# GpSimd's multiplication of q and k in four parts, three of VectorE's small steps in another order, and the values product in two pieces instead of three

## The reference

```python
x = x + 0.5 * ffn(layernorm(x))
x = x + attn(layernorm(x))
x = x + 0.5 * ffn(layernorm(x))

def attn(x):                                   # 16 heads of 64
    q, k, v = x @ Wq, x @ Wk, x @ Wv           # k and v get 4 memory rows in front
    q, k = l2norm(q), l2norm(k)
    dots = mix_heads(W_pre_th, q @ k.T * 10)   # a 16x16 mix over the heads
    dots = causal mask, then keep the 64 largest of each row
    attn = mix_heads(W_post_th, softmax(dots))
    out = (attn @ v) * head_scale * sigmoid(x @ Wg + bg)
    return out @ Wo
```

## Time and profile before

| | |
|---|---|
| median of 3 runs | 2192.57 us (2191.74 to 2193.78) |
| profiled execution, its own time | 2195.78 us |
| its span in the trace | 2194.0 us |
| busy in the span | PE 1996.8 (91%), PEld 1309.2, DVE 1698.7 (77%), ACT 1593.3 (73%), POOL 929.8 (42%) |
| mean granted TensorE clock | 0.963 of full speed |

### The profile page before, as it was taken

One profiled execution on the slowest core, in us unless ns is written; L12 is line 12 of the kernel. 1 busy time (PEld: TensorE's weight loads), 2 busy tenths in 40 slices (PEclk: granted clock), 3 DMA queues, 4 the chain that ended last, 5 costly groups with the idle time before them and its releaser, 6 DMA issues. The chain is left out here.

```text
span 2194.0 us, 56191 instructions
## 1 busy us (share of the span) xinstructions
PE 1996.8 (91%) x16059; PEld 1309.2 (60%) x16060; DVE 1698.7 (77%) x7474; ACT 1593.3 (73%) x4620; POOL 929.8 (42%) x2739
## 2 busy tenths in 40 slices
PE   6996689989998998999899989998999999984997
PEld 3433456676666666766666666666666766672433
DVE  6565389968996899689968986899699869964456
ACT  4442579967996899689868986898699778952542
POOL 3000555455545554555455546544664465321000
PEclk9997799999999999999999999999999999996998
DMA  6002012202220222112211221121122212202002
GB/s 185 3 0 91 12 48 52 62 16 53 64 53 24 53 65 46 28 46 65 46 27 46 65 46 27 46 65 46 28 54 57 46 28 64 68 15 92 0 1 77
DMA packets 113228, 104.82 MB, mean 48 GB/s; under 512 B 34448, under 2 KB 110864, under 8 KB 112912
## 3 DMA queue, kind: packets, MB, share of 16 engines
q1 hardware_dynamic: 108000, 96.65, 17.3%
q10 hardware_dynamic: 4912, 4.46, 0.6%
HBM read 19.14 MB, written 12.71 MB: 15 GB/s over the span
## 5 line engine op out<-in xcount | busy, mean ns | idle before, releaser
L1063 PE MATMUL bankC<-R,E 128*128 128x128 f32 x2560 | 347.9, 285 | 43.4 <-POOL R L1430 43.3
L1063 PEld LDWEIGHTS bankC<-R,E 128*128 128x128 f32 x2560 | 332.5, 199 | 82.5 <-POOL R L1430 49.3
L1047 PE MATMUL bankB<-raw,mixpre 128*128 128x76 f32 (+37 forms) x1024 | 339.5, 425 | 9.8 <-DMA raw<-SC 9.8
L1528 DVE TENSOR_SCALAR_CACHE_REDUCE S<-S,minus_thr 128x68 f32<-128x68 f32 (+56 forms) x456 | 217.6, 514 | 95.9 <-POOL minus_thr L1414 94.4
L1268 ACT ACTIVATE S<-bankB,aim_first 128x68 f32<-128x68 f32 (+56 forms) x456 | 229.5, 513 | 79.0 <-PE bankB L1047 78.5
L1405 POOL TENSOR_TENSOR S<-S,diagmask 128x8 f32<-128x8 f32 x512 | 112.8, 224 | 395.4 <-ACT S L1268 344.1
L1598 DVE SCALAR_TENSOR_TENSOR E<-S,limit,E 128x68 f32<-128x68 f32 (+56 forms) x456 | 242.7, 568 | 33.3 <-ACT E L1294 2.4
L1294 ACT ACTIVATE E<-S,nmax 128x12 f32<-128x12 f32 (+56 forms) x512 | 241.6, 535 | 0.4 <-POOL nmax L1445 0.4
L1089 PEld LDWEIGHTS bankM<-PT,V 128*64 128x64 f32 x5120 | 179.4, 138 | 98.1 <-issue 90.5
L1430 POOL TENSOR_SCALAR R<-mixpost,rinv 128x128 f32<-128x128 f32 x512 | 186.7, 377 | 116.7 <-DVE rinv L1602 116.5
L1047 PEld LDWEIGHTS bankB<-raw,mixpre 128*128 128x128 f32 x1024 | 156.9, 189 | 106.1 <-issue 84.4
(11 more groups left out here) (185 smaller groups left out, 4166.3 us busy)
## 6 DMA issues: line engine op xcount, KB each, us to landing
X_first<-in_L_attn_x_dram ACTq DMA_DIRECT2D x8, 512.0 KB, 10.0
x<-X_first SPq DMA_DIRECT2D x8, 512.0 KB, 2.9
xt<-x SPq DMA_DIRECT2D x32, 128.0 KB, 2.4
x<-xt SPq DMA_DIRECT2D x32, 128.0 KB, 2.5
X_last<-x SPq DMA_DIRECT2D x8, 512.0 KB, 7.0
out_dram<-X_last SPq DMA_DIRECT2D x8, 512.0 KB, 2.8
raw<-SC SPq DMA_DIRECT2D x8, 258.0 KB, 3.0
raw<-SC SPq DMA_DIRECT2D x8, 254.0 KB, 3.2
```

What stands on the lines that cost most here:

```text
L1047: last = nc.tensor.matmul(bankB[n % 2][:, 0:wide(n)], W.mixpre[:, :], raw[n % RAWS][:, 0:wide(n)], start=True, stop=True)
L1063: last = nc.tensor.matmul(bankC[n % 2][:, jb * P:(jb + 1) * P], E[n % EBUFS][:, jb * P:(jb + 1) * P], R[n % RBUFS][:, :], start=True, stop ...
L1528: nc.vector.tensor_scalar(row, row, minus_thr[:, col(n)], None, ALU.add, ALU.max, accum_out=rmax[:, col(n)]).then_inc(max_done, 1)
```

## The change

1. `norm` issues its multiplication in four instructions of four heads each ([128 x 256]) instead of one of [128 x 1024]; `turn_qk` waits for four times the count.
2. `flip` of a pair is issued between the two `row_max` of the turn instead of behind both.
3. The limits of a pair are two instructions [128 x 1], each waiting for its own `picked`, instead of one [128 x 2] waiting for both.
4. For pairs with g = 4, 8 or 12 the reciprocal is issued behind the first `row_max` of the next turn. In the other turns it stays at the end.
5. `attend` of a unit is issued in two pieces of four pairs of heads in the turns g mod 8 = 2 and 4, instead of pieces of 3, 3 and 2 pairs in the turns g mod 8 = 0, 2 and 4.

```diff
+NORM_PARTS = 4
...
             def turn_qk(j, i, what):
-                pe.wait_ge(qk_ready, 2 * j + i + 1)
+                pe.wait_ge(qk_ready, NORM_PARTS * (2 * j + i + 1))
...
-                if t and g % 8 < 6:
-                    attend(2 * t - 2 + g // 8, ((0, 1, 2), (3, 4, 5), (6, 7))[g % 8 // 2])
+                if t and 2 <= g % 8 < 6:
+                    attend(2 * t - 2 + g // 8, (range(4), range(4, 8))[g % 8 // 2 - 1])
...
-                nc.gpsimd.tensor_tensor(v, v, rn[:, i, :].unsqueeze(2).to_broadcast([P, H, DH]),
-                                        ALU.mult).then_inc(qk_ready, 1)
+                for part in range(NORM_PARTS):
+                    heads = slice(part * H // NORM_PARTS, (part + 1) * H // NORM_PARTS)
+                    nc.gpsimd.tensor_tensor(
+                        v[:, heads, :], v[:, heads, :],
+                        rn[:, i, heads].unsqueeze(2).to_broadcast([P, H // NORM_PARTS, DH]),
+                        ALU.mult).then_inc(qk_ready, 1)
...
+            def deferred(n0):
+                return n0 >= 0 and n0 % GPT in (4, 8, 12)
+
+            def sides_pair(n0):
...
+                    dve.wait_ge(side_done, ranked_upto(ranked[-1]))
+                    flipped[n0] = step(nc.vector.tensor_scalar(flip[:, cols], side[:, cols].bitcast(I32), 31, 0x7FFFFFFF,
+                                                               ALU.arith_shift_right, ALU.bitwise_or))
+
+            def invert_pair(n0):
+
+                both = (n0, n0 + 1)
+                dve.wait_ge(tk, kept_sum[n0])
+                if n0 >= RING:
+                    dve.wait_ge(R_ready, n0 - RING + 2)
+                nc.vector.reciprocal(rinv[:, ring(both)], rsum[:, ring(both)]).then_inc(E_ready, 2)
...
-                    dve.wait_ge(picked_done, ranked_upto(ranked[-1]))
-                    limited = step(nc.vector.tensor_tensor(
-                        limit[:, cols].bitcast(I32), key[:, parity(n0), in_batch(ranked)].bitcast(I32), flip[:, cols],
-                        ALU.bitwise_xor))
+                    for n in ranked:
+                        dve.wait_ge(picked_done, ranked_upto(n))
+                        at[n] = step(nc.vector.tensor_tensor(
+                            limit[:, col(n)].bitcast(I32), key[:, parity(n), n % GPB:n % GPB + 1].bitcast(I32),
+                            flip[:, col(n)], ALU.bitwise_xor))
...
-                if 2 <= n0 and n0 + 2 < NG:
+                more = 2 <= n0 and n0 + 2 < NG
+                if more:
                     row_max(n0 + 2)
+                if deferred(n0 - 2):
+                    invert_pair(n0 - 2)
+                sides_pair(n0)
+                if more:
                     row_max(n0 + 3)
...
                 select_pair(n0)
+                if not deferred(n0):
+                    invert_pair(n0)
```

More of the change, by code:

```diff
@@ L1540, in searched @@
                 return candidates(n) if is_split(n) else near[n % 2][:, 0:group_width(n)]
+            flipped, kept_sum = {}, {}
+            def deferred(n0):
+                return n0 >= 0 and n0 % GPT in (4, 8, 12)
+            def sides_pair(n0):
+                ranked = ranked_in(n0)
+                if ranked:
+                    cols = ring(ranked)
+                    dve.wait_ge(side_done, ranked_upto(ranked[-1]))
[7 more added lines that the diff above has]
+                nc.vector.reciprocal(rinv[:, ring(both)], rsum[:, ring(both)]).then_inc(E_ready, 2)
             def select_pair(n0):
@@ L1547, in select_pair @@
                 if ranked:
-                    cols = ring(ranked)
-                    dve.wait_ge(side_done, ranked_upto(ranked[-1]))
-                    flipped = step(nc.vector.tensor_scalar(flip[:, cols], side[:, cols].bitcast(I32), 31, 0x7FFFFFFF,
-                                                           ALU.arith_shift_right, ALU.bitwise_or))
-                    dve.wait_ge(tk, flipped)
+                    dve.wait_ge(tk, flipped[n0])
                     for n in ranked:
@@ L1595, in select_pair @@
                     if n in ranked:
-                        dve.wait_ge(tk, limited)
+                        dve.wait_ge(tk, at[n])
                         least = limit[:, col(n)]
@@ L1600, in select_pair @@
                         op0=ALU.is_ge, op1=ALU.mult, accum_out=rsum[:, col(n)]))
-                dve.wait_ge(tk, at[n0 + 1])
-                nc.vector.reciprocal(rinv[:, ring(both)], rsum[:, ring(both)]).then_inc(E_ready, 2)
+                kept_sum[n0] = at[n0 + 1]
             def mark_batch(i):
```

## The result

| | before | after |
|---|---|---|
| median of 4 runs, us | 2192.85 (2191.74 to 2193.78) | 2157.22 (2153.30 to 2158.68) |
| ratio of after to before | | 0.9835 (0.9823 to 0.9846) |
| span of the profiled execution, us | 2194.0 | 2155.7 |
| busy in the span: PE, DVE, POOL, us | 1996.8, 1698.7, 929.8 | 1964.2, 1658.7, 975.6 |
| mean granted TensorE clock | 0.963 | 0.972 |

Lines have moved by 1 to 24 (L1047 is now L1048, L1063 is L1064, L1089 is L1090, L1598 is L1622); the reciprocal went from L1602 to L1567.

A forecast was written before the change was run, and what follows sets the result against it. TensorE, busy for 91% of the span, was taken to bound the kernel. Terms: -8.6 - 5.2 + 18.6 - 13.0 - 4.8 + 1.6 + 0.5 = -10.9 us, giving 2181.7, rounded to 2181 us; range 2164 to 2198.

The forecast's parts named there:

- It adds and removes no matmul.: Values product on TensorE: two pieces keep the same matmuls and end in the same turn; no size given.
- (a): End of a batch: the `mix` comes earlier and removes VectorE's 1.08 us wait, 8.6 us gained over 8 batches.
- (b): Tile 0: R comes over 1 us earlier and TensorE's 0.74 us wait goes, 5.2 us gained in 7 batches.
- (c): Score step after turn g = 0's pairs leave: TensorE newly waits for ScalarE's copy of q, 18.6 us lost.
- (d): Turns 4 and 12: two more pairs run inside the score waits of turns 6 and 14, 13.0 us gained.
- VectorE's order: Three turns before R at a batch's end: limits and `flip` save 0.2 us each, deferral zero; 4.8 us gained.
- The rival that the operation count decides: VectorE: the limit's second instruction costs 0.1 us and hides nothing, `flip` gives nothing; +7.2 us, 2189 us; chance 0.12.
- GpSimd's parts: Multiplication in `norm`: VectorE gets in between parts but is not waited for; 1.6 us lost, bounds 0 and 5.
- The rival that VectorE doesn't get in: GpSimd's multiplication: VectorE can't start between its parts, and the 1.6 us cost goes; 2180 us; chance 0.10.
- The slower one: TensorE's score steps: the lost cover counts and the won one doesn't; +7.3 us, 2200 us; chance 0.14.
- the larger gain at the end of a batch: The earlier `mix` carries on over the turns; most of the 3.96 us wait goes; 2164 us; chance 0.17.

The follow-up runs named there:

- e1: The kernel before with only the values product (`attend`) in its two new pieces: 2173.09 us, ratio 0.9914.
- e5: The whole change without GpSimd's four parts (NORM_PARTS = 1), against the kernel before: 2153.68 us, ratio 0.9828.
- e4: The kernel before with 14 useless matmuls ahead of the turned block for which TensorE would stop: 2187.51 us, ratio 0.9976.
- e3: The kernel before with only GpSimd's multiplication in four parts: 2193.68 us, ratio 1.0001.
- e2: The kernel before with only the three edits on VectorE (`flip`, limits, deferred reciprocal): 2190.67 us, ratio 0.9990.

## Why the prediction was wrong

It was wrong in size: faster was right, 2181 was not (nor 2182, to which its 2181.7 rounds), and the mechanisms that it named are a small part of the gain, 5.1 of 31.3 us in six batches.

**"It adds and removes no matmul."** This sentence is the step that failed. True as it is, I priced the product by its pairs and took a pair to cost the same wherever it stands, and so the number of pieces, 24 a batch before and 16 after, had no price. It has one: about 0.3 us of TensorE's time a piece, 15.3 us in six batches and some 20 for all 62 pieces, half of the gain. The rows were there to see: in the earlier trace rows the `mix` of 128x476 took 1.88 us behind the product, and after it takes 1.77 behind the output projection.

**The clock.** No term had it. The mean clock of 0.963 stood in the table and the stop of 3.96 us was the centre of the argument, but I didn't look at what follows the stop: 6.8 us at 1.2 GHz, 2.4 us lost, 60% on top of the stop. Its part of the gain is about 1.8 us a batch, 10.9 us in the six batches, and it is why VectorE's edits give 19 us beside the pieces: of the 13.5 us that lie in the six batches (e1 to e5), 7.0 are less waiting and 6.3 the clock. The filler of e4 bounds what the clock takes before the change from below at 5 us. What decides whether it falls behind a stop of 2.4 us stays open.

**(a)** held in seven of the eight batches: 3.96 to 2.40 (about 2.3 was said), and the 1.08 us went. In the last the stop grew, from 4.30 to 5.29.

**(b)** failed: 1.00 instead of 0 us. R came earlier, and so did TensorE. In its place the wait for `raw` from the DMA went from 7.0 to 1.4 us, which I hadn't seen; it is as large as the 5.2 us that (b) claimed.

**(c)** held: 1.12, 0.99, 0.78 and 0.69 us where 0.9, 0.8, 0.5 and 0.5 were said, so 21.1 us more waiting for q instead of 18.6.

**(d)** held: 14.5 us less waiting for the scores instead of 13.0; the wait in tile 1 stays with 0.51 (under 0.45 was said).

**VectorE's order.** On the chain to R it gave 0.7 us a batch (stops of 3.10 in e1 and 2.40 after), where 0.6 was forecast, and 0.13 and 0.11 us a turn for `flip` and the limits, where 0.1 and 0.1 were. The rival that the operation count decides, with 0.3 us lost, fell. Groups by line over 440 to 1970 us of after (busy, mean ns, idle before), against the earlier trace rows:

```profile
L1622 DVE SCALAR_TENSOR_TENSOR E<-S,limit,E 128x492 f32<-128x492 f32 (+56 forms) x403 | 205.7, 546 | 6.5 <-ACT E L1295 2.6 <-issue 0.2
L1610 DVE TENSOR_TENSOR limit<-key,flip 128x1 int32<-128x1 int32 x403 | 61.2, 172 | 0.5 <-DVE picked L1604 0.2
L1567 DVE RECIPROCAL rinv<-rsum 128x2 f32<-128x2 f32 x227 | 37.2, 164 | 13.1
```

and E and the limits of before, 440 to 1990 us:

```profile
L1598 DVE SCALAR_TENSOR_TENSOR E<-S,limit,E 128x476 f32<-128x476 f32 (+56 forms) x405 | 217.6, 573 | 28.1 <-DVE limit L1586 1.9 <-ACT E L1294 0.2
...
L1586 DVE TENSOR_TENSOR limit<-key,flip 128x2 int32<-128x2 int32 (+1 forms) x206 | 39.5, 192 | 7.2
```

The limits cost 21.7 us more of busy time, and the idle time ahead of them, of E and of the reciprocal fell by 6.7 + 21.6 + 11.4 = 39.7. Net 18 us of VectorE on these three. The `row_max`, now with `flip` between them, are busy for 13.7 us more (191.8 to 205.5), and their idle time, nearly all of it a wait for the threshold, grew by 42.3 us (85.3 to 127.6).

**GpSimd's parts.** The mechanism was right (VectorE gets in, E takes 0.52 us in the midst of the parts, e3 gains nothing by it), and the price of 1.6 us is inside what e3 and e5 can tell from nothing. The rival that VectorE doesn't get in fell by the 0.52 us.

**The rivals.** The slower one fell with (d), by its own test. The one nearest in time, the larger gain at the end of a batch, gave 2164 by its own reason, an end of the batch with most of the stop gone. That reason fell too: the stop is 2.40 us, as in the forecast itself. It was near by luck.

## What to carry to other kernels

Before pricing a move on TensorE, list which part of the array each neighbour uses, and count the changes: here each stay in a 128\*64 product among 128\*128 work costs TensorE 0.29 to 0.34 us that no wait shows, so few long pieces beat many short ones, unless a piece covers a wait. Price a stop of TensorE with the clock behind it, and read how long the low stretch is. And measure a wait for its whole length: what a view shows is what the present cover leaves over.

## What the runs showed of the hardware that I had not expected

- A stop of 3.96 us of TensorE came with 6.8 us at 1.2 GHz (once 3.4), one of 3.1 to 3.4 us with 3.4 or 6.8, one of 2.40 us with 3.4 us or none, one of 0.74 us with none. In e2 a wait of 1.30 us came with 3.4. Useless matmuls in the stop made three kernels faster, by 5 to 8 us.
- A change of TensorE from one kind of 128\*128 matmul to another cost 0.00 us; into 128\*64 or 64\*64 it cost 0.09, and out of 128\*64 about 0.25 with the longer first `mix` behind it.
- Four multiplications of 128x256 took 2.50 us on GpSimd against 1.90 for one of 128x1024, in which VectorE could start between the parts.
- The whole multiplication holds more of VectorE once its order is changed: E's mean is 573 ns before, 600 in e5 and 546 with the parts. The 22 us of VectorE's busy time between the last two bought nothing.
